# Column tents of a two-layer deformable convolution: from GpSimd to ScalarE, with new written-out orders

## Time and profile before

| | |
|---|---|
| median of 3 runs | 174.35 us (172.06, 174.35, 175.23) |
| profiled execution: time / span | 174.54 us / 172.7 us |
| PE busy | 118.5 us (69%) |
| weight loads of PE | 77.0 us (45%) |
| DVE busy | 75.8 us (44%) |
| ACT busy | 63.9 us (37%) |
| POOL busy | 87.9 us (51%) |

### The profile page before, as it was taken

How to read it: one execution, slowest core, us unless ns; L and a number is a source line. 1 busy time by engine, 2 the same in 40 slices (tenths; PEclk the granted TensorE clock), 3 DMA queues, 4 the chain that set the end, 5 groups by cost and what they waited for, 6 DMA issues and landing times.

```text
span 172.7 us, 4571 instructions
## 1 busy us (share of the span) xinstructions
PE 118.5 (69%) x1953; PEld 77.0 (45%) x1953; DVE 75.8 (44%) x144; ACT 63.9 (37%) x101; POOL 87.9 (51%) x64
## 2 busy tenths in 40 slices
...
## 3 DMA queue, kind: packets, MB, share of 16 engines
...
HBM read 3.09 MB, written 0.59 MB: 21 GB/s over the span
## 4 chain that ended last, share of the span: by engine, by line
PE 41%; POOL 40%; issue 6%; DVE 4%; ACT 3%; DMA 3%; ACTq 1%; POOLq 0%; DVEq 0%
POOL xa L448 37%; PE ps L990 14%; PE ps L1006 10%; PE ps L927 8%; PE ps L905 5%; DMA full_m<-c_full 3%; ACT xa L525 1%; POOL rstd L438 1%; POOL bands L396 1%; PE ps L939 1%; DVE s L737 1%; ACT ya L506 1%; DVE xpad L665 1%; PE ps L921 1%; ACT res L544 1%
## 5 line engine op out<-in xcount | busy, mean ns | idle before, releaser
L448 POOL TENSOR_SCALAR xa<-xa 128x576 f32<-128x576 f32 x36 | 76.8, 2155 | 49.7 <-ACT xa L525 49.7
L737 DVE TENSOR_TENSOR s<-xa,ps 128x576 f32<-128x576 f32 x36 | 26.9, 753 | 36.4 <-POOL xa L448 31.1
L525 ACT ACTIVATE xa<-ps 128x576 f32<-128x576 f32 x36 | 22.6, 648 | 28.4 <-PE ps L959 20.9
L990 PE MATMUL ps<-s,xw 64*64 64x228 f32 (+5 forms) x480 | 27.6, 380 | 5.9 <-DVE s L737 5.9
L927 PE MATMUL ps<-xpad,w_o 64*64 64x288 f32 x288 | 25.1, 506 | 0.0
L990 PEld LDWEIGHTS ps<-s,xw 64*64 64x64 f32 x480 | 18.4, 142 | 14.3 <-DVE s L737 5.6
L959 PE MATMUL ps<-pos,soon 64*64 64x288 f16 x144 | 11.4, 339 | 12.7 <-DVE s L737 10.7
L533 ACT ACTIVATE val<-ps 128x504 f32<-128x504 f32 (+5 forms) x23 | 15.7, 724 | 11.3 <-PE ps L990 11.1
L972 PE MATMUL ps<-yh,soon 64*64 64x288 f16 x144 | 13.8, 364 | 8.2 <-DVE s L737 7.2
L1006 PE MATMUL ps<-val,w_d 64*64 64x288 f32 x288 | 19.3, 409 | 0.0
L927 PEld LDWEIGHTS ps<-xpad,w_o 64*64 64x64 f32 x288 | 15.4, 171 | 7.5 <-issue 5.1
...
## 6 DMA issues: line engine op xcount, KB each, us to landing
...
```

What stands on the lines that cost most here:

```text
L448: nc.gpsimd.tensor_scalar(v, v, 1.0, 1.0, ALU.min, ALU.subtract).then_inc(xu_ready, 1)
L525: nc.scalar.activation(xa[:, n % XA_BUFS, :, :], both(("x", n)), ACT.Abs).then_inc(frees("x", n), 1)
L737: nc.vector.tensor_tensor(s[m % 2][:, :, at:at + 9 * (ROWS - 1) + 1:9, b:b + W], xa[:, n % XA_BUFS, :, :].rearrange("p h (r c) -> p h r c" ...
L990: last = mm(to, xw[m % 2][64 * i:64 * i + 64, GRID * row + w, :], s[m % 2][64 * i:64 * i + 64, h, top:end, a:c], start=True, stop=True)
```

## The change

The column tent moves from POOL to ACT: `clamp` is now `column_tents`, a Relu with scale -1 and bias 1, that is max(0, 1 - |d|), in place, right behind or some instructions behind its `xabs` in ACT's order. Since it has no minus sign any more, the row tent gets a plus too: `yh` is copied with scale -1, and `yl` is -ya - yh. POOL's string keeps `pow`, `band` and `fpow` alone. The strings of all four engines are new; in them `vc` jobs are dealt out anew between ACT and DVE, conv.1, conv.2 and conv.3 have other jobs between their taps, w.0 and w.2 are interleaved with `x` and `y` jobs, and w.1 comes before the windows of stage 2.

```diff
-norm.0@0 conv.0.0@1 conv.0.1 conv.0.2 conv.0.3 conv.0.4 conv.0.5 conv.0.6 conv.0.7 conv.0.8 win.0.0@2
-win.0.1@3 yd.0.0@0 yd.0.1@1 x.0@2 x.1@3 norm.1@0 x.2@2 x.3@0 x.4@3 y.0@1 conv.1.0@2 conv.1.1 y.1@1
...
+norm.0@0 conv.0.0@1 conv.0.1 conv.0.2 conv.0.3 conv.0.4 conv.0.5 conv.0.6 conv.0.7 conv.0.8 norm.1@2
+win.0.0@3 win.0.1@0 conv.1.0@1 yd.0.0@2 yd.0.1@3 x.0@0 conv.1.1 conv.1.2 conv.1.3 x.1@2 x.2@3 x.3@0
+conv.1.4 conv.1.5 conv.1.6 conv.1.7 conv.1.8 x.4@2 x.5@3 y.0@1 y.1@0 y.2@1 y.3@0 y.4@2 y.5@1 x.6@3 x.7@0
+x.8@2 win.1.0@3 y.6@1 y.7@0 y.8@2 win.1.1@1 v.0.0@3 v.0.1@0 v.0.2@2 v.0.3@1 yd.1.0@3 v.0.4@0 v.0.5@2
+v.0.6@3 yd.1.1@1 x.9@0 x.10@2 w.0.0@3 w.0.1 y.9@0 w.0.2 y.10@2 w.0.3 y.11@1 w.0.4 x.11@0 w.0.5 w.0.6
+x.12@2 x.13@0 w.0.7 w.0.8 x.14@2 x.15@1 x.16@0 x.17@2 y.12@1 y.13@3 norm.2@1 y.14@3 y.15@0 y.16@1 y.17@2
+conv.2.0@3 conv.2.1 conv.2.2 conv.2.3 conv.2.4 v.1.0@0 v.1.1@1 v.1.2@2 conv.2.5 v.1.3@0 v.1.4@1 v.1.5@2
+v.1.6@0 conv.2.6 conv.2.7 conv.2.8 w.1.0@1 w.1.1 w.1.2 w.1.3 w.1.4 w.1.5 w.1.6 w.1.7 w.1.8 win.2.0@2
+yd.2.0@0 win.2.1@3 norm.3@1 yd.2.1@2 x.18@0 ym.2.0@3 ym.2.1@1 x.19@2 x.20@0 x.21@3 conv.3.0@2 x.22@1
+conv.3.1 conv.3.2 conv.3.3 y.18@0 conv.3.4 conv.3.5 conv.3.6 conv.3.7 conv.3.8 y.19@3 x.23@0 win.3.0@1
+win.3.1@3 x.24@2 y.20@0 y.21@1 y.22@3 x.25@0 y.23@1 x.26@2 y.24@3 y.25@0 y.26@1 flag@2 yd.3.0@2 yd.3.1@3
+x.27@2 x.28@0 ym.3.0@3 v.2.0@1 v.2.1@2 v.2.2@0 v.2.3@3 v.2.4@1 v.2.5@2 v.2.6@0 x.29@3 x.30@1 x.31@2
+y.27@0 y.28@3 y.29@1 y.30@0 ym.3.1@3 x.32@2 w.2.0@1 y.31@3 w.2.1 y.32@2 x.33@0 w.2.2 x.34@3 w.2.3 w.2.4
+y.33@0 y.34@2 x.35@3 w.2.5 w.2.6 y.35@0 w.2.7 w.2.8 v.3.0@3 v.3.1@2 v.3.2@0 v.3.3@1 v.3.4@3 v.3.5@2
+v.3.6@0 fm.0@1 w.3.0@3 w.3.1 w.3.2 fv.0@2 w.3.3 w.3.4 w.3.5 w.3.6 w.3.7 w.3.8 fm.1@0 fv.1@1
...
 DVE_ORDER
+stats.0.0 stats.0.1 aggr.0 group.0 stats.1.0 normed.0 stats.1.1 aggr.1 group.1 clip.0 omax.0 normed.1
+pos.0 yu.0.0 yu.0.1 yl.0.0 clip.1 mul.0 mul.1 mul.2 mul.3 mul.4 mul.5 yl.0.1 omax.1 mul.6 mul.7 mul.8
+pos.1 vc.0.1 vc.0.3 yu.1.0 vc.0.5 yl.1.0 yu.1.1 mul.9 yl.1.1 mul.10 mul.11 mid.0.0 mid.0.1 aggr.2 mul.12
+mul.13 group.2 mul.14 normed.2 mul.15 mul.16 mul.17 vc.1.1 vc.1.4 vc.1.6 mix.2 clip.2 omax.2 pos.2
+mid.1.0 mid.1.1 aggr.3 yu.2.0 group.3 ymul.2.0 normed.3 yu.2.1 ymul.2.1 yl.2.0 mul.18 mul.19 yl.2.1
+mix.3 clip.3 omax.3 mul.20 mul.21 mul.22 mul.23 oall pos.3 far mul.24 mul.25 mul.26 yu.3.0 yu.3.1
+ymul.3.0 vc.2.0 vc.2.2 vc.2.3 yl.3.0 vc.2.6 mul.27 mul.28 mul.29 ymul.3.1 mul.30 mul.31 yl.3.1 mul.32
+mul.33 mul.34 mul.35 last.0.0 last.0.1 fmean.0 vc.3.1 vc.3.3 vc.3.6 fspread.0 fvar.0 fscale.0 fsum.0
+last.1.0 last.1.1 fmean.1 fspread.1 fvar.1 fscale.1 fsum.1
...
 ACT_ORDER
+off.0 high.0 wc.0.0 wc.0.1 yabs.0.0 yabs.0.1 xabs.0 yh.0.0 clamp.0 xabs.1 clamp.1 xabs.2 clamp.2 off.1
+xabs.3 clamp.3 yh.0.1 xabs.4 clamp.4 xabs.5 clamp.5 xabs.6 clamp.6 xabs.7 xabs.8 clamp.7 clamp.8 wc.1.0
+high.1 wc.1.1 vc.0.0 vc.0.2 yabs.1.0 vc.0.4 yh.1.0 vc.0.6 xabs.9 xabs.10 yabs.1.1 clamp.9 yh.1.1
+clamp.10 xabs.11 clamp.11 xabs.12 xabs.13 xabs.14 xabs.15 clamp.12 clamp.13 clamp.14 xabs.16 xabs.17
+clamp.15 clamp.16 clamp.17 vc.1.0 vc.1.2 vc.1.3 vc.1.5 off.2 sig.2 high.2 wc.2.0 yabs.2.0 wc.2.1
+yabs.2.1 xabs.18 clamp.18 xabs.19 clamp.19 yh.2.0 xabs.20 xabs.21 clamp.20 clamp.21 xabs.22 clamp.22
+yh.2.1 off.3 sig.3 xabs.23 clamp.23 wc.3.0 wc.3.1 high.3 xabs.24 xabs.25 xabs.26 clamp.24 clamp.25
+clamp.26 yabs.3.0 yabs.3.1 xabs.27 xabs.28 clamp.27 clamp.28 vc.2.1 yh.3.0 vc.2.4 vc.2.5 xabs.29 xabs.30
+clamp.29 xabs.31 clamp.30 clamp.31 xabs.32 yh.3.1 clamp.32 xabs.33 xabs.34 clamp.33 clamp.34 xabs.35
+clamp.35 sum.2.0 sum.2.1 vc.3.0 vc.3.2 vc.3.4 vc.3.5 relu.0 sum.3.0 sum.3.1 relu.1
...
 POOL_ORDER
+pow.0 band.0 pow.1 band.1 pow.2 band.2 pow.3 band.3 fpow.0 fpow.1
...
-            def clamp(n):
-                wait_taken(pool, "x", n)
-                v = xa[:, n % XA_BUFS, :, :]
-                nc.gpsimd.tensor_scalar(v, v, 1.0, 1.0, ALU.min, ALU.subtract).then_inc(xu_ready, 1)
...
-                nc.scalar.activation(yh[m % 2][:, c, :], ya[:, c, :], ACT.Copy).then_inc(yh_ready, 1)
+                nc.scalar.activation(yh[m % 2][:, c, :], ya[:, c, :], ACT.Copy, scale=-1.0).then_inc(yh_ready, 1)
...
+            def column_tents(n):
+                wait_taken(act, "x", n)
+                v = xa[:, n % XA_BUFS, :, :]
+                nc.scalar.activation(v, v, ACT.Relu, bias=1.0, scale=-1.0).then_inc(xu_ready, 1)
...
-                nc.vector.tensor_tensor(yl[m % 2][:, c, :], ya[:, c, :], yh[m % 2][:, c, :], ALU.subtract)\
+                nc.vector.scalar_tensor_tensor(out=yl[m % 2][:, c, :], in0=ya[:, c, :], scalar=-1.0,
+                                               in1=yh[m % 2][:, c, :], op0=ALU.mult, op1=ALU.subtract)\
```

More of the change, by code:

```diff
@@ L65 @@
 PE_ORDER = """
-norm.0@0 conv.0.0@1 conv.0.1 conv.0.2 conv.0.3 conv.0.4 conv.0.5 conv.0.6 conv.0.7 conv.0.8 win.0.0@2
-win.0.1@3 yd.0.0@0 yd.0.1@1 x.0@2 x.1@3 norm.1@0 x.2@2 x.3@0 x.4@3 y.0@1 conv.1.0@2 conv.1.1 y.1@1
-conv.1.2 conv.1.3 x.5@0 conv.1.4 conv.1.5 conv.1.6 conv.1.7 conv.1.8 y.2@3 y.3@1 y.4@0 y.5@2 x.6@3 x.7@1
-x.8@3 y.6@0 y.7@1 y.8@2 win.1.0@3 v.0.0@0 yd.1.0@1 yd.1.1@2 v.0.1@3 v.0.2@0 v.0.3@1 x.9@2 v.0.4@3
-v.0.5@0 v.0.6@2 y.9@1 win.1.1@3 w.0.0@0 w.0.1 w.0.2 w.0.3 w.0.4 w.0.5 w.0.6 w.0.7 w.0.8 x.10@2 x.11@1
@@ L81 @@
+x.27@2 x.28@0 ym.3.0@3 v.2.0@1 v.2.1@2 v.2.2@0 v.2.3@3 v.2.4@1 v.2.5@2 v.2.6@0 x.29@3 x.30@1 x.31@2
+y.27@0 y.28@3 y.29@1 y.30@0 ym.3.1@3 x.32@2 w.2.0@1 y.31@3 w.2.1 y.32@2 x.33@0 w.2.2 x.34@3 w.2.3 w.2.4
+y.33@0 y.34@2 x.35@3 w.2.5 w.2.6 y.35@0 w.2.7 w.2.8 v.3.0@3 v.3.1@2 v.3.2@0 v.3.3@1 v.3.4@3 v.3.5@2
+v.3.6@0 fm.0@1 w.3.0@3 w.3.1 w.3.2 fv.0@2 w.3.3 w.3.4 w.3.5 w.3.6 w.3.7 w.3.8 fm.1@0 fv.1@1
 """
 DVE_ORDER = """
-stats.0.0 stats.0.1 aggr.0 group.0 stats.1.0 normed.0 stats.1.1 aggr.1 clip.0 omax.0 pos.0 yu.0.0
@@ L85 @@
[L85 to L89, removed]
```

18 lines of the change are left out of this document (2 added, 16 removed).

## The result

| | before | after |
|---|---|---|
| median | 174.0 us (172.06 to 175.23, 4 runs) | **135.02 us** (133.97 to 135.54, 4 runs) |
| profiled execution: time / span | 174.54 / 172.7 us | 135.26 / 133.5 us |

The ratio is 0.7781, with a 95% interval from 0.7692 to 0.787. The direction and the main mechanism, POOL's tent leaving the chain, were right; the size was not. Runs of one kernel differ by up to about 3%, and those over 1.5% above its fastest are left out of the ratios, while medians here are over all runs and spans are each of the one profiled execution.

What follows compares the result with a forecast made beforehand. POOL's column clamp, 37% of the chain, was taken as the bound. Marks summed step by step to 141.2 us; 3.9 for low clock made the span 145.1, and 1.84 around it gave 147.0, range 139.5 to 158.

Steps and rivals of the forecast that it cites:

- step 3: From stage 0's last product through v.0, w.0 and statistics: conv.2 starts at 58.2 us, not at 74.31.
- step 4: From conv.2's start through v.1, w.1 and norm.3: conv.3 starts at 81.2 us against 102.5.
- step 5: From conv.3's start through win.3 and taps: the last product of stage 2 ends at 98.8 us.
- step 6: v.2, y.27 to y.35, w.2, four x, a row mask: the last product ends at 117.3 us, before 142.56.
- step 7: v.3 6.2 us, its last copy 0.8, w.3 with the two small reductions 5.1: w.3 ends at 129.4.
- allowance for a low clock: Half of the low-clock price added for conv.1 to conv.3: 3.9 us, making the span 145.1.
- B: Rival: each tap becomes a round trip of its PSUM slot, 1.6 us instead of 1.27: 159 us; chance 0.20.
- C: Rival: in-order queues stand on one another, slower than before: 212 us, or 180 at 2.3 a tap; chance 0.02.
- step 2: conv.1, off.1 until 28.7 us, six ACT pairs and yh 8.1, product 0.75: stage 0's last product at 37.6.
- the price of x and y: On PE, each y job was taken at 0.5 us and each x job at about 0.3.
- Rival A: PE keeps full clock, no slips: 143.0 us, down to 139.5 if y costs half in places; chance 0.18.
- The end: From w.3's end to the end of the span, as before: 11.8 us, giving 141.2.

Runs made afterwards that it cites:

- e10: The changed kernel with each x and y job running its matmuls twice over: 141.29 us, ratio 0.8069.
- e12: The changed kernel with all nine taps of w.2 moved behind y.35, the last y job: 139.03 us.
- e13: The changed kernel run once more, unaltered, as a yardstick: 133.95 us, ratio 0.7729.
- e14: The changed kernel with fm.0 behind w.3.3 and fv.0 behind w.3.5, as in the old order: 136.41 us, ratio 0.7833.
- e4: The changed kernel with its orders, but the 36 column tents on DVE, each right ahead of its product: 148.42 us, ratio 0.8602.

## Why the prediction was wrong, step by step

The marks, predicted and measured:

| mark | predicted | measured | miss of the step |
|---|---|---|---|
| first row spread | 21.5 | 21.8 | +0.3 |
| last product of stage 0 | 37.6 | 37.6 | -0.3 |
| conv.2 starts (step 3) | 58.2 | 57.3 | -0.9 |
| conv.3 starts (step 4) | 81.2 | 79.0 | -1.3 |
| v.2 starts (step 5) | 98.8 | 94.4 | -2.2 |
| last product (step 6) | 117.3 | 110.7 | -2.2 |
| w.3 ends (step 7) | 129.4 | 123.0 | +0.2 |
| end | 141.2 | 133.5 | -1.3 |
| allowance for a low clock | 3.9 | 0 | -3.9 |

That is 11.6 us of span; the time around the span was 1.8 as taken.

**Right.** *Column tent:* 682 ns, and DVE's waits for ACT are 3.8 us, where over 20 would have meant B or C. *Signs:* the four large yl instructions take 752 ns, and no mark shows their cost. *POOL:* out of the chain. Steps 1 and 2 fell within 0.3 us, and step 7 within 0.2.

**Luck in step 2.** Its 37.6 is exact, its path is not. off.1 ended at 28.04, not 28.7, and the six pairs took 7.7 us, not 8.1; but the last three products, not one, came behind them, since they had stood 1.44 us for a y that was behind win.1.0 on PE:

```profile
35.51 2.08 DVE L738 TENSOR_TENSOR s<-xa,ps 128x576 f32<-128x576 f32 x3 [1.44 <-PE ps L973]
```

**The step that failed: the price of x and y (steps 3, 5 and 6).** This is the largest term that was mis-sized, 5.3 of the 11.6 us. The prediction took y at 0.5 from a row at the low clock and x at about 0.3, for which the earlier trace rows have no row, and put them one behind another on PE. At full clock a y job is 0.24 and an x job 0.12 in the chain after. w.0 with its three y and three x, 7.1 in step 3, took 5.8. e10 doubled the two prices, and came within 1.4 us of the five predicted marks named there; it made steps 3, 5 and 6 longer by 1.5, 1.7 and 1.6 us, where the prediction had missed by 0.9, 2.2 and 2.2. So y was priced from a row at 1.2 GHz beside convs, v and w from rows at 2.4 GHz, and x by the length of one job alone, where jobs in a row cost less than half of that. (Step 3's remark that POOL had nine clamps there, 19.4 us, is a misreading on which no term rests: up to conv.2's start POOL was busy for 16.8 us, rstd included.) The right prices stood in the chain of the kernel before, in a stretch whose clock was 0.98:

```profile
50.09 0.12 PE ps L959 x4
...
52.67 0.24 PE ps L972 x8
```

In step 6 the form of the sum failed as well. It adds up PE's jobs, w.2's 4.9 among them; e12 took w.2 out, and the last product ended at 110.5 as before, so ACT's round of the taps sets that stretch and PE's jobs fit into it. At 0.5 a y job PE's sum came out the longer of the two, which is what e10 brought about.

**The allowance for a low clock.** Half of the price that a conv paid over the full clock was taken, for three convs. In the profiled execution of the changed kernel conv.1, conv.2 and conv.3 ran at full clock. In the repeat (e13) the first five taps of conv.2 took 3.35 and not 2.67 us, so some allowance was due, of 0.7 and not 3.9. (The 7.26 us of the earlier trace rows isn't a whole conv at 1.2 GHz either: its clock was 0.5 up to 80 us and 1.00 behind.) Rival A had it right in kind, and its own low end, 139.5, was still 4.5 us above the time, since it halved y alone, in steps 2, 3 and 6, and kept the old end.

**Step 4** missed by 1.3 in small pieces: conv.2 with v.1 took 10.3 of 10.9, and w.1, win.2 with yd, and mid.1 the rest. Adding the lengths of rows counts the overlap of neighbours twice, since one run of matmuls begins before the last has ended (57.39 + 2.67 = 60.06, while v.1 starts at 59.82). e10 left this step alone (+0.1), so it is not the price of x and y. These pieces were read, not tested.

**The end** was carried over as 11.8 and took 10.5: the two small reductions sit earlier in w.3 in the new order, so pair 0's relu is over before pair 1's sum. e14 put them back and got 11.6. The prediction named this piece "as before" without going through the new strings there. (The old end is 11.74, which the sum has as 11.8.)

**Rivals B and C** had the old wait come back as a round trip of the slots; ACT's waits for products were 0.5 us. What came nearest is e4, where the queue of DVE did it (8.5 us). The tents without the orders come to 156 us, the orders alone to 162: the last 8.5 us need both.
